# Gathers of the segment-sum passes: index copies by ScalarE and one GpSimd wait for two regions, in place of direct indices and waits on GpSimd

## The reference

```python
# network 1, once:
m = relu(x[src]);  agg = segment_sum(m, dst, N);  h = (1 + eps) * x + agg        # then two linear layers
# network 2, four steps:
for _ in range(4):
    trans = einsum('nd,tod->tno', h, W_edge) + b_edge[:, None, :]
    msg = trans[etypes, src];  a = segment_sum(msg, dst, N);  h = gru_cell(a, h, ...)
```

## Time and profile before

| what | us |
|---|---|
| median of two runs | 12443.72 |
| the profiled execution's own time | 12435.64 |
| its span, first to last instruction | 12433.7 |
| POOL busy | 6378.4 |
| gathers of the sum passes, busy (3140) | 618.2 + 2482.8 |

### The profile page before, as it was taken

The page is one execution under the profiler, slowest core; times in us unless marked ns, Lnnn a source line. Parts: engine busy times, 40 slices in busy tenths (PEclk is TensorE's granted clock), DMA queues, the critical chain, the costliest instruction groups (busy, mean ns, idle before and its releaser), DMA issues. The chain is left out here.

```text
span 12433.7 us, 154586 instructions
## 1 busy us (share of the span) xinstructions
PE 6625.2 (53%) x36192; PEld 5643.9 (45%) x36193; DVE 4969.4 (40%) x11746; ACT 2217.8 (18%) x4249; POOL 6378.4 (51%) x6364
## 2 busy tenths in 40 slices
PE   4555687555687555686334333533533343355555
PEld 3555674555574555674333232333323333334443
DVE  4444664444674444673223221322312232235555
ACT  1222453222453222452000000000000000011111
POOL 2555432555432555431664566366366636625553
PEclk6777898777798777797556665655755575577777
DMA  2333321333331333330111211111111111112221
GB/s 78 112 113 114 101 85 51 113 111 113 97 90 47 113 113 115 99 89 20 45 45 32 72 45 45 57 45 45 53 50 45 44 59 45 45 39 78 77 77 56
DMA packets 698397, 893.93 MB, mean 72 GB/s; under 512 B 148418, under 2 KB 443212, under 8 KB 698131
## 3 DMA queue, kind: packets, MB, share of 16 engines
q0 software_dynamic: 198368, 429.61, 13.5%
q1 hardware_dynamic: 498474, 461.96, 11.8%
q10 hardware_dynamic: 1416, 0.86, 0.0%
HBM read 698.72 MB, written 193.14 MB: 72 GB/s over the span
## 5 line engine op out<-in xcount | busy, mean ns | idle before, releaser
L851 POOL DMA_INDIRECT l_sums_ring<-table_typed,tile_idx x2512 | 2482.8, 988 | 1773.3 <-issue 727.3
L960 PE MATMUL psum<-l_sums_ring,select 128*128 x7840 | 1669.2, 393 | 3039.8 <-DVE acc L941 1086.8
L821 POOL DMA_INDIRECT acc<-table_x,index x2016 | 2045.3, 1015 | 2166.5 <-DVE index L816 1541.0
L960 PEld LDWEIGHTS psum<-l_sums_ring,select 128*128 128x128 f32 x7840 | 1513.3, 293 | 3198.5 <-issue 3195.3
L941 DVE TENSOR_TENSOR acc<-acc,psum 128x128 f32 x980 | 280.5, 286 | 3179.6 <-remote 2414.8
L1078 PE MATMUL psum<-ident,select 128*128 128x128 f32 x2016 | 435.4, 355 | 1493.1 <-ACT l_scores_mixT L1018 507.6
L1053 DVE TENSOR_TENSOR acc<-l_scores_key,psum 128x512 f32<-128x512 f32 x504 | 345.9, 686 | 1776.8 <-ACT l_scores_key L1026 1331.8
L1078 PEld LDWEIGHTS psum<-ident,select 128*128 128x128 f32 x2016 | 295.5, 180 | 1569.1 <-issue 947.7
L821 POOL DMA_INDIRECT l_pass_ring<-table_kv,index x672 | 675.5, 1005 | 635.5 <-issue 264.4
L851 POOL DMA_INDIRECT l_sums_ring<-table_x,tile_idx x628 | 618.2, 984 | 634.6 <-ACTq L78 335.0
L925 DVE SCALAR_TENSOR_TENSOR select<-dst_all,pair_start,iota_row 128x512 f32<-128x512 f32 x980 | 732.5, 748 | 524.8 <-issue 407.9
(11 more groups left out here) (343 smaller groups left out, 10753.4 us busy)
## 6 DMA issues: line engine op xcount, KB each, us to landing
acc<-in_edge_attr_dram SPq DMA_DIRECT2D x2016, 64.0 KB
rows_dram<-l_scores_mixT SPq DMA_DIRECT2D x504, 256.0 KB
l_values_ring<-rows_dram SPq DMA_DIRECT2D x504, 256.0 KB
table_typed<-l_rows_rows SPq DMA_DIRECT2D x40, 1024.0 KB, 4.3
l_sums_ring<-table_typed,tile_idx POOLq DMA_INDIRECT x2512
acc<-table_x,index POOLq DMA_INDIRECT x2016
l_pass_ring<-table_kv,index POOLq DMA_INDIRECT x672
table_x<-l_rows_rows SPq DMA_DIRECT2D x40, 256.0 KB, 2.3
```

The source lines that it names most:

```text
L821: pool.indirect_dma_start(out=ring[:, at, u, :], out_offset=None, in_=table, in_offset=bass.IndirectOffsetOnAxis(ap=index[:, at % REGIONS, ...
L851: pool.indirect_dma_start(out=ring[:, k % TILE_RING, u, :], out_offset=None, in_=table, in_offset=at).then_inc(gathered[k % REGIONS], 16)
L960: ins = pe.matmul(sums(k), select[:, k, u, :], rows, start=u == 0, stop=u == GROUP - 1)
```

## The change

ScalarE now takes over the waits and hands POOL the indices. For each region it loads its number from `room_at` (from the ninth on), waits for region k - 4 to have landed and for the room, and copies four columns of `tile_idx` into place k % 4 of `index`, incrementing `p_index`. POOL runs a loop of 19 turns over 8 regions, and five regions behind it; it waits once for each two regions, until both are copied, and then issues eight gathers through `gather` (L821), as the other passes do.

```diff
-        def gathers_by_tile(pool, ring, table, base):
-            rooms = []
-            for k in range(TILE_REGIONS):
-                if k >= REGIONS:
-                    pool.wait_ge(gathered[k % REGIONS], landed(k // REGIONS - 1, base[k % REGIONS]))
-                    pool.sem_inc(gather_go, 1)
-                if k >= TILE_RING:
-                    if not rooms:
-                        rooms = by_step(pool, room_at, k - TILE_RING, min(TILE_RING, TILE_REGIONS - k), PAIRS, 1)
-                    pool.wait_ge(p_summed, rooms.pop(0))
-                    pool.sem_inc(gather_go, 1)
-                for u in range(GROUP):
-                    at = bass.IndirectOffsetOnAxis(ap=tile_idx[:, k * GROUP + u:k * GROUP + u + 1], axis=0)
-                    pool.indirect_dma_start(out=ring[:, k % TILE_RING, u, :], out_offset=None, in_=table, in_offset=at
-                                            ).then_inc(gathered[k % REGIONS], 16)
+        def gathers_by_tile(pool, ring, table):
+            def pair(first, at, n):
+                pool.wait_ge(p_index, first + (at + n))
+                pool.sem_inc(gather_go, 1)
+                for k in range(at, at + n):
+                    gather(pool, ring, table, k)
+            with pool.Fori(0, TILE_TURNS) as i:
+                for at in range(0, TILE_RING, 2):
+                    pair(i * TILE_RING, at, 2)
+            rest = TILE_REGIONS - TILE_TURNS * TILE_RING
+            for at in range(0, rest, 2):
+                pair(TILE_TURNS * TILE_RING, at, min(2, rest - at))
...
+                    @b.scalar
+                    def _(act):
+                        def ask(i, r, reused=True):
+                            if reused:
+                                room, = by_step(act, room_at, region_of(i, r) - TILE_RING, 1, PAIRS, 1)
+                            if not (isinstance(i, int) and i == 0):
+                                act.wait_ge(gathered[r], landed(i - 1, base[r]))
+                            if reused:
+                                act.wait_ge(p_summed, room)
+                            act.copy(index[:, r, :], tile_idx[:, bass.ds(step_of(i, r), GROUP)]).then_inc(p_index, 1)
+                        first, turns_of = TILE_RING // REGIONS, TILE_REGIONS // REGIONS
+                        for i in range(first):
+                            for r in range(REGIONS):
+                                ask(i, r, reused=False)
+                        with act.Fori(first, turns_of) as i:
+                            for r in range(REGIONS):
+                                ask(i, r)
+                        for r in range(TILE_REGIONS % REGIONS):
+                            ask(turns_of, r)
```

More of the change, by code:

```diff
@@ L903, in pair_turns @@
                     body(PAIR_TURNS - 1)
-                with block(name, p_landed, p_selected, p_summed, p_added) as b:
+                with block(name, p_index, p_landed, p_selected, p_summed, p_added) as b:
                     @b.gpsimd
                     def _(pool):
-                        gathers_by_tile(pool, ring, table, base)
+                        gathers_by_tile(pool, ring, table)
                     @b.sync
```

## The result

The changed kernel took 12599.99 us (median of two runs, 12593.51 to 12606.47) against 12443.72: 156 us more, where I had said 126 us. The record lists ten executions of it in all, 12578.42 to 12650.47 with a median of 12627, which is 183 us more. The recorded ratio, 1.0145 with a 95% interval of 1.0109 to 1.0181, fits these ten; the medians of two alone give 1.0126. So the change makes the kernel slower, by 1.3 to 1.5%, and by less than the 2% from which on I call a difference clear. Its profiled execution took 12596.53 us, 161 more than that of before, with a span of 12594.7.

A forecast was written before the change was run, and what follows sets the result against it. No engine over 53% busy; in the five sum passes POOL's gathers and its pauses for ring room, held by select, matmuls and add, bound the time. Longer pauses add 125 us to 12444: 12570 us said, range 12300 to 12950.

The forecast's parts named there:

- Which stages and what bounds them: Five sum passes: POOL's gathers, their gaps and 38 pauses of 2.9 us a pass, waiting for room in the ring.
- Gathers out of the small tile, in a loop: POOL's gathers out of `index`: taken as 0, with 0 to 85 us for gathers and -20 to 63 for the loop.
- The start: First gather of a pass waits for two index copies: taken as 0, covered by VectorE clearing `acc`; uncovered 2 us.
- The hand-over: At a pause, POOL's gather follows ScalarE's copy instead of the sum directly: 0.32 us more for each pause.
- The wait for two regions: POOL goes on only when both regions have room: 0.7 us a pause, a quarter of 2.8; bounds 0 and 2.8.
- The slower rival: Sum passes: half the pauses wait a full region more, 2.0 us a pause on the mean; 12850 us, chance 0.30.
- The load between the two: ScalarE's load for the second region behind the first's copy: 0.57 us in a quarter of pauses, 0.1 us a pause.
- The sum: Sum passes: pauses grow 1.1 us to 4.0, 35 instead of 38; 25 us a pass taken, 125 us in all.
- "faster": With the wait on ScalarE, sums come when matmuls end and no pause is left: 11890 us, chance 0.12.
- "Nothing is lost": Sum passes: the chain, not POOL, is the bound and uses any longer pause: 12444 us, chance 0.20.

The follow-up runs named there:

- e6: The changed kernel, but POOL waits for one region's index copy at a time: 12448.11 us against 12376.16 before, ratio 1.0057.
- e11: The kernel before, unedited, against itself, as yardstick with a second profile: 12377.54 us, ratio 0.9999.
- e7: The kernel before, but POOL itself waits for room for two regions, nothing on ScalarE: 12445.39 us against 12376.16 before, ratio 1.0052.
- e9: The changed kernel, but ScalarE loads the four room numbers of a turn at once: 12591.43 us against 12471.70 before, ratio 1.0108.
- e8: The changed kernel again, unedited, on a chip with late sums: 12616.33 us against 12471.70 before, ratio 1.0126.
- e1: The changed kernel again, unedited, on a chip without late sums: 10635.96 us against 10630.43 before, ratio 1.0006.
- e5: The kernel before, but every two regions POOL also waits until its last issued region has landed: 12778.19 us against 12450.94 before.
- e10: The kernel before, but VectorE makes each select three pairs ahead instead of one: 12396.28 us against 12471.70 before, ratio 0.9941.
- e12: The kernel before with selects three pairs ahead, and POOL silent every four regions until its last region has landed: 12369.81 us against 12384.82, ratio 0.9990.
- e4: The changed kernel, but ScalarE loads a turn's four room numbers at once, on the chip without late sums: 10632.07 us against 10630.43 before, ratio 1.0004.

## Why the prediction was right

*Which stages and what bounds them*: right. The sum passes moved, and in them the pauses above all; a pass takes 942 us on the mean, the number foretold (938, 940, 928, 948 and 954 to the start of its last gather; 1 us more to its end). That a pause is a wait for room was read from one pause in the prediction. It holds for nearly all: 174 of the 189 pauses of before end 0.6 to 0.8 us behind the start of an add.

*Gathers out of the small tile, in a loop*: taken at 0, right. The mean gather is 979 ns against 988, the gap 0.30 us in both. The 1015 ns of the score pass, my upper bound, belong to that pass (1012 ns after).

*The start*: 0, right. The first gathers start 7.3 us later over the five passes and take 7.3 us less (4.9 us in four of them, against 6.6), since they end when VectorE has cleared `acc`; the first `select` and the first add stand where they stood against it. A load of ScalarE's table (1.28 us) that I had not seen coming stands ahead of the first index copy in four passes, under the same cover.

*The hand-over*: 0.32 us a pause foretold, 0.28 measured (e6 against e11), and 70 us in all. But I let the chain take back a part of every longer pause by fewer pauses; in e6 their number did not fall (193 and 191). It fell with the wait for two regions: 144 in e7, 160 in the changed kernel.

*The wait for two regions*: 0.7 us foretold, 0.8 measured, and "a quarter of the pauses" fits 37 of 149. The reason I gave for the rest was wrong: not that sums come in twos, for where POOL waits for the first region the second comes 3.56 us later on the mean, often 5.7 with VectorE's load in it; but that three quarters of the pauses begin with the first region's room already there. The step itself was sized too low, 2.8 us for a region. I had counted it from 6236.32 on, over a pair that was finished already in the silence; the three intervals from 6237.19 to 6245.34 give 3.4 us. The slower rival had half of the pauses in its sum, and no fewer pauses, and that is where it failed.

*The load between the two*: I had taken POOL's 0.57 us; ScalarE's is 0.28. The term of 0.1 us a pause (some 15 us) and the 25 us of e9 agree as far as the runs tell, which isn't far.

*The sum*: 35 pauses of 4.0 us foretold, 32 of 4.27 measured, 140 and 137 us a pass. This is closer than its parts, and in part luck: a pause grew by 1.42 us where I had 1.1, and their number fell by six where I had three. From 111 to 140 I had 29 us a pass and took 25, for pauses that merge; the measured excess is 29.0. The 30 us that the forecast lacks against the median of two are this rounding down (20 us), and some ten of the 16 us outside the passes that I don't read. Against the median of the ten it lacks 57 us, and against the 145 of e8 19 us; the runs place the cost no closer than that. Two terms that I had not set cancel: the gathers behind the first ones are 20 us shorter in all, and the tails of the passes 19 us longer, since at a pass's end the last sums are as late as any and the chain lies further behind.

*The rivals*: "faster" is refuted by the trace after (ScalarE has the wait, VectorE's unexplained time is 503.6 us in the first pass) and by e6. "Nothing is lost" is refuted where sums are late. On the chip of e1, though, it is what happens, for a reason that I did not have: there are no pauses. That finished sums come up to some 20 us late while gathers run was right for the trace that I had and wrong as a property of the kernel; on that chip the forecast of +1.0% would have been wrong in its mechanism. And "reported late" is a reading: the ends of matmuls are modelled in these profiles, so whether the sum or only its report is late is not shown.

## What to carry to other kernels

Before a hand-over is moved or a wait widened, ask how often that wait ends last and what is needed in between: each pause costs the difference, and the rest of the change is free. A wait for two things at once costs only where the first of them is the one waited for, and then a whole step of the chain behind it. When a wait is for late reports and not for work, giving the late engine more finished work per silence can help (here selects three pairs ahead, -0.6%). And look at a second chip before believing that a wait belongs to the kernel.

## What the runs showed of the hardware

- Sums of TensorE reached the engines that wait for them up to some 20 us late while POOL's indirect gathers ran, on the chips of the first two kernels, of e5 with e8 to e10, of e6 and e7, and of e11 and e12; on the chip of e1 to e4 never. The same program takes 12444 and 10630 us, a difference of 1813 us, more than eleven times the 156 us of the change. What makes the chips differ stays open.
- In the trace of before, sums were seldom late just behind a pause of POOL: of 106 that were ready, with VectorE free for them, in the first 3 us behind one, one was waited for over 1 us, of 96 at 9 to 12 us 0.88. ("Ready" goes by the modelled ends of the matmuls.) With a silence every 10 us (e5) it was 0 of 940 or so behind a silence.
- A load of one number takes 0.28 us on ScalarE's queue (of four 0.31, e9), of eight 0.57 on POOL's and 1.85 on VectorE's.
- In e8 each pass is longer than the one before it (936 to 956 us), and in the first trace of the changed kernel the last two are the longest (949 and 955 against 929 to 941), while in before they don't grow, nor in e9 from the first to the last (938 and 941). This is unexplained.
